# Cross-attention scores on two column tiles of the array

## The chip, the cores and the metric

The kernel runs on one core of a Trainium2 chip. The metric is the device time of one execution in microseconds (us), the median of several runs.

## The reference

One perceiver layer in float32 on `x` of 16 sequences x 64 tokens x 512: cross-attention to a context, then self-attention, then a feed-forward block with a mixture of small experts. Each adds to its input and takes a layer norm of it. The change is in the cross-attention:

```python
queries = (q @ Wq.T).reshape(B, Sq, 32, 128).transpose(0, 2, 1, 3)
keys    = (k @ Wk.T).reshape(B, Skv, 8, 128).transpose(0, 2, 1, 3)
values  = (v @ Wv.T).reshape(B, Skv, 8, 128).transpose(0, 2, 1, 3)
queries, keys = _rope(queries), _rope(keys)
keys, values = (jnp.repeat(t, 4, axis=1) for t in (keys, values))
scores = jnp.einsum('bhqd,bhkd->bhqk', queries, keys) * 128 ** -0.5
scores = jnp.where(causal, scores, finfo.min)
attn = softmax(scores); ctx = attn @ values; out = ctx @ Wd.T
```

The mask is causal, so of the context only the first 64 tokens matter.

## The kernel before

Everything lies in SBUF; the engines run hand-written programs that meet at semaphores. The cross-attention has 16 units: for each of 8 KV heads, two halves of 8 sequences. `phase(u, ...)` is one unit's program on an engine. A loop runs it 14 times (two to an iteration), unit 14 follows in a variant `"last"`, and unit 15 is taken apart among the work around it.

In unit `u`, TensorE (`pe`) first makes the scores (`scores_x`, chunk 0 and 1, four sequences each), then alternates the projections of unit `u+1` (`project`, in `proj_x`, `three`, L1110) with the rest of unit `u`: transposes of the softmax weights (`p_transposes`, L1149), weights times V (`pv_x`, L1156 and L1157), and at the end four output projections (`out_x`, L1110 too). Most products there are three `F32R` matmuls of values split in a high and a low part. The scores are plain float32: `qr` (queries after rope, 128 x 8 x 4 x 64: dimension, sequence, query head of the group, token) is the stationary operand, `kr` (keys) the moving one. A pair of query heads makes the 128 stationary columns, so that the result of one matmul has 128 partitions (2 heads x 64 query tokens) and 64 key columns. A chunk fills 512 columns of one PSUM bank, `sc[:, c, :]`:

```python
last = pe.matmul(sc[:, c, (2 * b + hp) * S:(2 * b + hp + 1) * S],
                 qr[h][:, bb, 2 * hp:2 * hp + 2, :], kr[h][:, bb, :],
                 start=True, stop=True)
```

After a chunk the semaphore `scored` goes up by one. VectorE (`dve`) adds the mask (`mask_max`, L787) and takes the maximum (L790), GpSimd (`pool`) subtracts it (L410), ScalarE (`act`) takes the exponential (L563), VectorE sums (L794), GpSimd normalises (L415) and raises `normed`, for which TensorE waits before `p_transposes`. The second chunk's exponential stands on ScalarE behind the copy of the next unit's first projection (`swap_halves`, L538 and L539). GpSimd also does the rope (L398, L403) and splits weights (L377); VectorE the rope's cosine part (L780), the output addition (L838) and the low parts of V (L804).

In the variant `"last"` the two chunks of unit 15 are scored between the output projections of unit 14 (after the second and after the fourth), while VectorE takes the statistics for the next layer norm (L735, L738) among its output additions.

In the self-attention behind it, `pv_s` (L1330) multiplies with 64 stationary columns, `vc[h][:, 2*c+b, t, :]`, for `t` = 0 and 1 in turn, into the partitions `64*t` to `64*t+63` of a bank. It also is plain float32, with 128 moving columns, eight records in a group, 32 groups. The matmuls around it are L1306 (scores), L1319 (transposes), L1261 (projections) and, in the last groups, L1402 (output projection).

Of the kernel before, what the change touches and what calls it, by code (L numbers as in the profile page):

```python
# [26 lines left out]
B, S, D = 16, 64, 512  # L27
# [32 lines left out]
def build(nc, x, ctxT, w_x, w_s, w_o, w_b, w_ag, w_eb, consts, bias_cols, bias_rows, b_thr, out):  # L60
    es = ExitStack()
    with es:
# [3 lines left out]
        def sb(stack, name, shape, dt=F32):  # L66
            return stack.enter_context(nc.sbuf_tensor(name, shape, dt))
# [27 lines left out]
        kr = [sb(xs, f"kr{i}", [P, HB, S]) for i in range(2)]  # L95
        qr = [sb(xs, f"qr{i}", [P, HB, REP, S]) for i in range(2)]
# [64 lines left out]
        def pb(name):  # L161
            return es.enter_context(nc.psum_tensor(name, [P, 2, 512], F32))
        pj, sc, tp, pv = pb("pj"), pb("sc"), pb("tp"), pb("pv")
# [925 lines left out]
        def _(pe):  # L1089
# [47 lines left out]
            def scores_x(u, h, c):  # L1137
                for b in range(4):
                    bb = 4 * c + b
                    for hp in range(2):  # L1140
                        last = pe.matmul(sc[:, c, (2 * b + hp) * S:(2 * b + hp + 1) * S],  # L1141
                                         qr[h][:, bb, 2 * hp:2 * hp + 2, :], kr[h][:, bb, :],
                                         start=True, stop=True)
                last.then_inc(scored, 1)

            def p_transposes(u, c):
# [48 lines left out]
            def phase(u, h, g, nxt):  # L1195
# [13 lines left out]

                pe.wait_ge(rope, 5 * u + 5)  # L1210
                scores_x(u, h, 0)
                scores_x(u, h, 1)
                project(0)
                project(1)
# [15 lines left out]
                for i in range(4):  # L1230
                    if i % 2 == 0:
                        pe.wait_ge(pv_lo, 2 * u + i // 2 + 1)
                    if i < 2:
                        pe.wait_ge(pj_act, XT * n + 5 + i)
                    pe.wait_ge(pj_dve, PD_LN1 + 4 * u + i - 1)
                    out_x(u, i)
                    if nxt == "last" and i in (1, 3):
                        if i == 1:
                            pe.wait_ge(rope, 5 * n + 5)
                        scores_x(n, 1, i // 2)  # L1240
# [179 lines left out]
            for n in range(N_SS):  # L1420
                v, c = n // SCH, n % SCH
# [79 lines left out]
            for i in range(NT):  # L1501
                pe.wait_ge(hw_done, i + 1)
                last = pe.transpose(sc[:, i // 4, (i % 4) * P:(i % 4 + 1) * P], hw[:, i, :], ident)
# [73 lines left out]
```

## Time and profile before

| | |
|---|---|
| median of 3 runs | 805.54 us (805.36 to 805.68) |
| span of the profiled execution | 802.9 us |
| TensorE matmuls busy | 780.4 us (97%) |
| TensorE weight loads busy | 643.9 us (80%) |
| VectorE, GpSimd, ScalarE busy | 511.5, 467.9, 390.6 us |
| mean granted clock of TensorE | 0.985 |

PE is TensorE's matmuls, PEld its loads of the stationary operand, DVE VectorE, ACT ScalarE, POOL GpSimd. The span goes from the first to the last instruction; the runs' time has 2.6 us more. A matmul's record is longer than the time after which the next one starts, since matmuls overlap in the array; so the distance of starts tells what one costs. A form such as `128*128 128x64` is rows and columns of the stationary operand, and then what is streamed past it. A plain float32 matmul shows as two loads and two matmul records (a transpose as one of each).

### The profile page before, as it was taken

Reading aid. Unit: us, or ns where it says so; the run is one execution under the profiler, and the core shown is the slowest. Engines: PE = TensorE matmul, PEld = TensorE weight load, DVE = VectorE, ACT = ScalarE, POOL = GpSimd, SP = SyncE. Lnnn points to the kernel's source line nnn. Section 1 sums busy time; section 2 is a strip of 40 time slices with the busy share of each in tenths; the row PEclk is TensorE's granted clock in tenths of the full one; section 3 lists DMA queues with packets and bytes.
Section 4 is the critical chain, followed back from the end, with each engine's and each line's share of the span. In section 5 each row is a group of like instructions: output and inputs, shape, how many; then the busy total and the mean of one; then the engine's idle time right before and its main releaser. Section 6 shows DMA issues by size and latency. Waiting matters only on the chain.

```text
span 802.9 us, 11770 instructions
## 1 busy us (share of the span) xinstructions
PE 780.4 (97%) x4112; PEld 643.9 (80%) x4112; DVE 511.5 (64%) x927; ACT 390.6 (49%) x692; POOL 467.9 (58%) x363
## 2 busy tenths in 40 slices
PE   6899999999999999999999999999799999999998
PEld 4688888888888888888888888888688777777786
DVE  6866465655655565565555566466857777779855
ACT  3546436453543735455373454537254666564220
POOL 4538546764754675485376458637543687865350
PEclk9889999999999999999999999999799999999999
DMA  8102101200210120030012003001101110001002
GB/s 296 53 2 78 53 1 52 78 0 0 78 52 0 52 78 0 0 97 34 0 52 78 0 3 124 3 0 41 40 1 52 40 51 2 2 19 63 14 1 105
DMA packets 11338, 34.09 MB, mean 42 GB/s; under 512 B 1456, under 2 KB 1584, under 8 KB 11312
## 3 DMA queue, kind: packets, MB, share of 16 engines
q1 hardware_dynamic: 11312, 33.75, 12.8%
q8 instruction: 16, 0.26, 0.1%
q14 instruction: 10, 0.08, 0.0%
HBM read 31.65 MB, written 2.10 MB: 42 GB/s over the span
## 4 chain that ended last, share of the span: by engine, by line
PE 90%; DVE 6%; issue 2%; ACT 1%; POOL 1%; DMA 1%; SPq 0%; ACTq 0%; POOLq 0%
PE pj L1110 53%; PE pj L1261 8%; PE sc L1141 7%; PE sc L1306 3%; PE pv L1330 2%; PE tp L1319 2%; PE pv L1156 2%; PE pv L1157 2%; PE tp L1149 2%; DVE sm L755 1%; PE pj L1402 1%; PE pj L1465 1%; PE tp L1134 1%; DVE al L857 1%; PE pv L1465 1%
## 5 line engine op out<-in xcount | busy, mean ns | idle before, releaser
L398 POOL TENSOR_TENSOR sw<-sw,cst 128x512 f32<-128x512 f32 x79 | 109.4, 1385 | 62.5 <-ACT sw L539 62.3
L410 POOL TENSOR_TENSOR sm<-sm,mx 128x512 f32<-128x512 f32 x64 | 67.3, 1052 | 133.9 <-DVE mx L790 133.9
L563 ACT ACTIVATE sm<-sm 128x512 f32<-128x512 f32 x64 | 40.5, 633 | 149.5 <-POOL sm L410 149.1
L538 ACT ACTIVATE sw<-pj 64x512 f32<-64x512 f32 x80 | 47.7, 596 | 127.0 <-DVE t L780 126.7
L1110 PE MATMUL pj<-xh,wqh 128*128 128x512 f32 x252 | 103.3, 410 | 0.0
L1110 PE MATMUL pj<-wdh,ch 128*128 128x512 f32 x256 | 101.8, 398 | 0.2 <-issue 0.2
L415 POOL TENSOR_TENSOR sm<-sm,rz 128x512 f32<-128x512 f32 x64 | 66.9, 1045 | 58.4 <-DVE rz L797 58.4
L1110 PE MATMUL pj<-wdh,cl 128*128 128x512 f32 x256 | 99.8, 390 | 0.0
L1110 PE MATMUL pj<-wdl,ch 128*128 128x512 f32 x256 | 99.7, 389 | 0.0
L1110 PE MATMUL pj<-xh,wql 128*128 128x512 f32 x252 | 99.6, 395 | 0.0
L1110 PE MATMUL pj<-xl,wqh 128*128 128x512 f32 x252 | 99.3, 394 | 0.0
L838 DVE TENSOR_TENSOR X<-X,pj 128x512 f32<-128x512 f32 x60 | 41.2, 686 | 73.7 <-PE pj L1110 73.2
L403 POOL TENSOR_TENSOR qr<-t,sw 128x512 f32<-128x512 f32 x63 | 82.0, 1301 | 4.9
L815 DVE TENSOR_TENSOR pt<-tp,pt 64x512 fp32r<-64x512 f32 x64 | 44.1, 689 | 57.0 <-ACT pt L557 56.5
L787 DVE TENSOR_TENSOR sm<-sc,cst 128x512 f32<-128x512 f32 x64 | 44.2, 690 | 42.7 <-PE sc L1306 22.2
L780 DVE TENSOR_TENSOR t<-pj,cst 128x512 f32<-128x512 f32 x80 | 55.1, 689 | 21.1 <-PE pj L1110 18.4
L1261 PE MATMUL pj<-xh,ws 128*128 128x512 f32 x192 | 67.8, 416 | 0.7 <-ACT xh L505 0.7
L1141 PEld LDWEIGHTS sc<-kr,qr 128*128 128x128 f32 x512 | 61.5, 197 | 4.6 <-DVE qr L889 3.4
L1141 PE MATMUL sc<-kr,qr 128*128 128x64 f32 x512 | 60.9, 278 | 3.1 <-DVE qr L889 3.1
L794 DVE TENSOR_REDUCE zs<-sm 128x8 f32<-128x512 f32 x64 | 43.5, 679 | 30.5 <-ACT sm L563 29.9
L377 POOL TENSOR_TENSOR wql<-raw,wqh 128x1024 fp32r<-128x1024 f32 x24 | 57.4, 2398 | 9.3 <-ACT wqh L505 9.1
L823 DVE TENSOR_TENSOR cl<-pv,ch 128x256 fp32r<-128x256 f32 x128 | 45.2, 415 | 24.6 <-ACT ch L568 24.6
(201 smaller groups left out, 1759.0 us busy)
## 6 DMA issues: line engine op xcount, KB each, us to landing
raw<-in_w_x SPq DMA_DIRECT2D x40, 512.0 KB, 4.0
qr<-in_ctxT SPq DMA_DIRECT2D x4, 512.0 KB, 7.1
X<-in_x SPq DMA_DIRECT2D x4, 512.0 KB, 7.5
raw<-in_w_s SPq DMA_DIRECT2D x4, 512.0 KB, 3.6
out<-X SPq DMA_DIRECT2D x8, 256.0 KB, 2.1
raw<-in_w_s SPq DMA_DIRECT2D x4, 256.0 KB, 3.1
raw<-in_w_o SPq DMA_DIRECT2D x2, 512.0 KB, 3.7
raw<-in_w_b SPq DMA_DIRECT2D x2, 512.0 KB, 6.2
```

Source lines behind the costliest of these rows:

```text
L377: pool.tensor_tensor(lo, src, hi.bitcast(F32), ALU.subtract).then_inc(wlo, 1)
L398: pool.tensor_tensor(sw[par][:, :].rearrange("p (b s) -> p b s", s=S), sw[par][:, :].rearrange("p (b s) -> p b s", s=S), rep(cst[:, C_SIN: ...
L403: pool.tensor_tensor(o, t1[par][:, :].rearrange("p (b s) -> p b s", s=S), sw[par][:, :].rearrange("p (b s) -> p b s", s=S), ALU.add).then_ ...
L410: pool.tensor_tensor(s3, s3, per_group(mx[:, c, :], 8), ALU.subtract).then_inc(subbed, 1)
L415: pool.tensor_tensor(s3, s3, per_group(rz[:, c, :], 8), ALU.mult).then_inc(normed, 1)
L538: act.activation(sw[par][0:64, :], src[64:128, :], ACT.Copy)
L780: dve.tensor_tensor(t1[par][:, :].rearrange("p (b s) -> p b s", s=S), pj[:, bank, :].rearrange("p (b s) -> p b s", s=S), rep(cst[:, C_COS: ...
L787: dve.tensor_tensor(s3, sc[:, c % 2, :].rearrange("p (n s) -> p n s", s=S), mask3, ALU.add).then_inc(masked, 1)
L823: last = dve.tensor_tensor(cl[:, r, cs].rearrange("p (b q) -> p b q", q=S), pv[:, :, :].rearrange("p a (b r q) -> p (a b) r q", b=2, r=REP ...
L1110: last = pe.matmul(o, w, r, start=(m == 0), stop=(m == n - 1))
L1141: last = pe.matmul(sc[:, c, (2 * b + hp) * S:(2 * b + hp + 1) * S], qr[h][:, bb, 2 * hp:2 * hp + 2, :], kr[h][:, bb, :], start=True, stop= ...
L1261: last = pe.matmul(pj[:, k % 2, :], ws[t][:, part // 2, i, c], (xl if part == 1 else xh)[:, i, tok], start=(m == 0), stop=(m == 3 * KT - 1))
```

## The change

Each score matmul on a pair of heads becomes two, one for each head `r`: 64 stationary columns, whose result goes to the partitions `64*r` to `64*r+63` of the same columns of the same bank. The data, the order of chunks and all semaphores stay.

```diff
                 for b in range(4):
                     bb = 4 * c + b
                     for hp in range(2):
-                        last = pe.matmul(sc[:, c, (2 * b + hp) * S:(2 * b + hp + 1) * S],
-                                         qr[h][:, bb, 2 * hp:2 * hp + 2, :], kr[h][:, bb, :],
-                                         start=True, stop=True)
+                        for r in range(2):
+                            last = pe.matmul(sc[64 * r:64 * r + 64, c, (2 * b + hp) * S:(2 * b + hp + 1) * S],
+                                             qr[h][:, bb, 2 * hp + r, :], kr[h][:, bb, :],
+                                             start=True, stop=True)
                 last.then_inc(scored, 1)
```

## Rows read from the trace of the kernel before

**Rows 1.** The page: engines (busy, share, records) and the chain that ended last

```profile
PE 780.4 (97%) x4112; PEld 643.9 (80%) x4112; DVE 511.5 (64%) x927; ACT 390.6 (49%) x692; POOL 467.9 (58%) x363
...
PE pj L1110 53%; PE pj L1261 8%; PE sc L1141 7%; PE sc L1306 3%; PE pv L1330 2%; PE tp L1319 2%; PE pv L1156 2%; PE pv L1157 2%; PE tp L1149 2%; DVE sm L755 1%; PE pj L1402 1%; PE pj L1465 1%; PE tp L1134 1%; DVE al L857 1%; PE pv L1465 1%
```

**Rows 2.** Waits of PE, whole span (total us, times, longest), the second of 16

```profile
PE sc L1141 <- DVE qr L889: 3.1, 1, 3.1
```

**Rows 3.** Records by line: count, duration ns min/median/max, first and last start

```profile
L1141 PEld LDWEIGHTS sc<-kr,qr x512: 187/192/337, 41.6 to 569.0; 128*128 128x128 f32 x171
L1141 PE MATMUL sc<-kr,qr x512: 217/275/422, 41.6 to 569.1; 128*128 128x64 f32 x171
...
L1330 PEld LDWEIGHTS pv<-pts,vc x256: 132/136/137, 617.2 to 740.1; 128*64 128x64 f32 x128
L1330 PE MATMUL pv<-pts,vc x256: 272/273/323, 617.2 to 740.2; 128*64 128x128 f32 x128
...
L1306 PE MATMUL sc<-kb,qm x128: 377/379/454, 591.3 to 730.0; 128*128 128x256 f32 x128
```

**Rows 4.** Timeline of PE around a unit's scores: start, length from first to last

```profile
114.03 0.39 PE L1110 MATMUL pj<-wdh,cl 128*128 128x512 f32 x1
114.26 3.68 PE L1141 MATMUL sc<-kr,qr 128*128 128x64 f32 x32
...
118.06 0.40 PE L1110 MATMUL pj<-al,wqh 128*128 128x512 f32 x1
```

**Rows 5.** Windows, records of L1330 alone; (x) counts those running in it

```profile
617.20:617.26 0.06, 0.04 (x2) 0.04 (x2) 1.00 0.00 0
617.26:617.37 0.11, 0.11 (x2) 0.11 (x4) 1.00 0.00 0
617.37:617.40 0.03, 0.03 (x4) 0.03 (x4) 1.00 0.00 0
617.48:617.52 0.04, 0.04 (x6) 0.04 (x4) 1.00 0.00 0
```

**Rows 6.** Timeline of PE around the last group of L1330

```profile
739.46 0.40 PE L1402 MATMUL pj<-woh,al 128*128 128x512 f32 x1
739.79 0.66 PE L1330 MATMUL pv<-pts,vc 128*64 128x128 f32 x8
...
740.72 0.39 PE L1402 MATMUL pj<-wol,ah 128*128 128x512 f32 x1
```

**Rows 7.** Windows, all engines: us, busy PE PEld DVE ACT POOL, granted clock, DMA

```profile
43.20:50.00 6.80, 6.80 (x27) 6.22 (x27) 5.88 (x10) 0.63 (x1) 2.29 (x3) 0.50 0.00 1
148.96:183.67 34.71, 34.71 (x181) 29.27 (x180) 18.81 (x33) 14.73 (x29) 18.49 (x15) 1.00 0.09 30
567.48:591.30 23.82, 19.62 (x93) 15.74 (x92) 15.48 (x28) 11.98 (x21) 7.58 (x7) 0.79 0.03 9
591.00:803.00 212.00, 205.00 (x1185) 161.31 (x1183) 157.21 (x330) 95.90 (x160) 123.40 (x104) 1.00 0.10 33
```

**Rows 8.** Timeline of DVE at the first chunk of unit 15

```profile
561.86 0.18 DVE L738 BATCH_NORM_AGGREGATE mv<-stats 128x2 f32<-128x6 f32 x1
562.14 0.69 DVE L787 TENSOR_TENSOR sm<-sc,cst 128x512 f32<-128x512 f32 x1
```

**Rows 9.** Timelines of DVE, POOL and PE in the unit at 148.96 us

```profile
149.16 0.69 DVE L838 TENSOR_TENSOR X<-X,pj 128x512 f32<-128x512 f32 x1 [1.33 <-PE pj L1110]
150.89 0.69 DVE L787 TENSOR_TENSOR sm<-sc,cst 128x512 f32<-128x512 f32 x1 [1.04 <-PE sc L1141]
...
155.17 1.05 POOL L415 TENSOR_TENSOR sm<-sm,rz 128x512 f32<-128x512 f32 x1
159.32 1.04 POOL L415 TENSOR_TENSOR sm<-sm,rz 128x512 f32<-128x512 f32 x1 [3.11 <-DVE rz L797]
...
158.13 0.60 PE L1149 MATMUL tp<-cst,sm 128*128 128x128 f32 x4
161.35 0.27 PE L1149 MATMUL tp<-cst,sm 128*128 128x128 f32 x1
```

## The prediction, as put down before the result

> **What bounds the kernel now.** I read the page first, then the chain of waits, the PE groups and their waits, then single stretches. The page and its chain say that TensorE is the bound: it is busy 97% of the span, and of the chain that ended last the projections (L1110) hold over half and the cross scores (L1141) 7% [rows 1]. The waits of PE are 16, of 3.2 us at most, nearly all at the start and around 570 us; the score line has one of 3.1 us, before the first unit, and none later [rows 2]. So inside the 15 regular units between 41 and 560 us every TensorE microsecond saved comes off the end, as long as the softmax chain keeps up. 802.9 us of the time is the span; the median of the runs is 805.54, so 2.6 us lie around the span, and the sum below takes its differences off both alike.
>
> **What the scores cost now.** A unit (one KV head, one half of the tokens) has 16 score matmuls. Each is f32 and shows as two loads and two matmul records, so the line has 512 records over 16 units [rows 3]. In a regular unit the last projection record before them starts at 114.03 us, the 32 score records start from 114.26 on, and the second projection record after them starts at 118.06 [rows 4]. That whole passage is 118.06 - 114.03 = 4.03 us. Inside it the 32 records last 3.68 us with 0.275 for the last one, so their pitch is (3.68 - 0.275)/31 = 0.110 us; leaving out the first, which had its load ready, it is 0.112. The moving side has only 64 columns. A record with 128 moving columns lasts 0.273 us, one with 256 0.379 [rows 3], so 128 columns stream in 0.106 us and 64 in 0.053. A pitch of 0.112 is therefore not the stream's: it is the load's of 128 columns. This is where there is something to win.
>
> **What the change does, step by step.** It issues twice the score matmuls (1024 records), each with a 64-column load, alternately on the left and the right half of the array. Nothing else is changed: no DMA, no wait, no PSUM bank, the same values in the same places, and one increment of the semaphore behind the last matmul of a chunk.
>
> 1. *The load.* 64 columns take 0.136 us as a record where 128 take 0.192 [rows 3], that is 0.056 less. From 0.112 the pitch of one half's loads becomes 0.056 to 0.057; the stream is 0.053, so both fit.
>
> 2. *Do the halves run side by side?* The same form already runs in the kernel: L1330 (self-attention times V) alternates the halves in the same way, f32, 64 columns loaded, 128 moving. The counts in narrow stretches show it: two matmuls and two loads start by 617.26, no matmul more until 617.37, two more by 617.40 and two more by 617.52 [rows 5]. Matmuls start in pairs, a pair per 0.109 us (0.66 us for eight records [rows 6] less 0.273 for the last is 0.38 for three steps; the first, into the halved array, takes 0.16, the others 0.11). One stream of 128 columns takes 0.106, so two streams run at once. The loads come in pairs as well. I take this for the new form: a pair per 0.057 us, 32 pairs a unit in place of 32 single records at 0.112. That the two halves would be side by side with 64 moving columns too is the step that the trace doesn't show. Its bounds are 0.053 (streams alone) and 0.113 (the loads of the halves one after the other, 2 x 0.0565).
>
> 3. *Entering and leaving the halved array.* From the last projection record before an L1330 group to the second record after it the trace has 739.46 to 740.72, 1.26 us for four pairs [rows 6]. Four streams of 0.106 are 0.43, and in projections without a switch the two records around would take 0.23 each. So some 0.4 us of it is switching. The Trainium skill says the same in a rule that speaks against this change (TensorEngine Tiling (Array Packing), Key Properties): changing the tiling mode drains TensorE. The trace agrees: 739.46 to 739.79 is 0.33 us where 0.23 is usual for such a record. It changes no number here, since the 1.26 us holds it.
>
> 4. *Sum of a unit.* 1.26 us for four pairs; each of these streams 64 columns instead of 128, 4 x (0.109 - 0.057) = 0.21 less; 28 more pairs at 0.057 are 1.60. That makes 2.65 us against 4.03: 1.38 us less per unit. With the pitch at its lower bound 0.053 it is 1.50 less.
>
> 5. *How many units.* 15 pass straight from projections into both chunks of scores and back. The first of them runs in a stretch at the lower clock, 1.2 GHz (granted clock 0.50 from 43.2 to 50.0 us [rows 7]). I count it as 1.38 like the others: if the stretch keeps its place, what is saved appears at its end at 2.4 GHz; at most it gives 2.8. The last unit's scores are written between the output projections (560.21 and 567.48), and there DVE is behind: its statistics end at 562.04, the mask of the scores starts at 562.14 [rows 8]. Earlier scores gain 0.1 us and no more; both half groups then leave PE waiting instead (0.5 us each).
>
> **Sum:** 15 x 1.38 + 0.1 = 20.8 us. 802.9 becomes 782.1, and 805.5 becomes 784.7.
>
> **What is late next.** In the unit at 148.96 us the first chunk's scores are masked at 150.89 by DVE and normalised by POOL until 156.22; PE asks for them at 158.13 [rows 9]: 1.9 us spare. The first chunk would be ready for the mask at about 150.2 (0.1 us for the switch, 0.11 to the second pair, 14 x 0.057, 0.22 for the last record), 0.7 earlier than now, while PE comes 1.38 earlier: 1.2 us remain. DVE is free in time, since its output addition ends at 149.85. The second chunk is normalised until 160.36 and wanted at 161.35: 1.0 spare. Its chain waits for the exponential behind ACT's copy of the next projection, which moves with PE, so 1.0 remains. The output addition that frees the bank for the second projection ends at 149.85, and that projection would start at about 153.9. Nothing in a unit comes to bind. DVE is busy 18.8 of 34.7 us of a unit, POOL 18.5, ACT 14.7 [rows 7], far from the new 33.3.
>
> **The rivals.**
>
> *The halves don't overlap (slower).* If the two loads of a pair go one after the other the pitch of a pair is 0.113 us, as dear as a whole record now, and the switch comes on top: 2.65 + 32 x 0.056 = 4.44 us, 0.41 more than now, times 16 gives 6.6 us, 812 us. It decides at a pitch of 0.057 + 1.38/32 = 0.100 us. For it: only four pairs in a row are ever seen. Against it: the loads that start in pairs [rows 5]. 0.09.
>
> *The instructions don't come fast enough (slower).* The new form wants two loads and two matmuls every 0.057 us, the densest seen is the same number per 0.109 [rows 5]; were 0.109 a limit of the issue, a unit would take 2.65 + 32 x 0.052 = 4.31 us, 0.28 more than now, x 16 = 4.5, 810 us. In rows 6 eight matmuls and eight loads start in 0.66 - 0.273 = 0.38 us without such a limit showing, but they may have been queued beforehand. 0.05. The Trainium skill has a rule of this sort (TensorE: Matmul & The Clock Gate, What happens when you issue a matmul): where the sequencer decodes matmuls in microcode it spends about 62 ns on each. By it a pair would take 0.124 us and the time would be an estimated 818; the trace's pairs at 0.109 don't agree with it, if they were not queued.
>
> *Partly overlapping.* Pairs hold their pitch only while the queue is full of them, or a conflict costs some 0.03 us each: 0.085 a pair makes a unit 2.65 + 32 x 0.028 = 3.55 us, 0.48 less than now, 15 x 0.48 = 7.2, 798 us. The range of such cases is 788 to 803. 0.12.
>
> *The change does nothing,* a pitch of a pair between 0.097 and 0.103: 0.03. For it there is no row, it is where the cases meet.
>
> *A softmax wait takes over.* PE would stop before the transposes of a chunk's weights (L1149) for POOL's normalised scores. The first chunk's would have to come 1.2 us later than worked out, the second's 1.0; each 0.1 us beyond that costs 1.5 us in all, and with 0.3 the time is 789. Against it is that every operation of the chain keeps its length: 0.02, 786 to 795.
>
> *The forecast:* 0.69.
>
> **The clock.** Through the stretch with 32 L1330 groups the granted clock is 1.00 [rows 7], so work on half arrays keeps 2.4 GHz. After the idle time near 570 us the clock is at 1.2 GHz for a while (0.79 on average from 567.48 to 591.30). There PE will idle about 1 us more than now. A longer slow stretch could cost up to 3 us, a luckier one give 2. This and the first unit are the main spread of the forecast itself: 781 to 788.
>
> **How the numbers follow.** The likeliest is 784.7. The lower end: pitch 0.053 (1.8 us less) and a lucky clock, 781. Upwards the range takes in the clock's 3 us and most of the partial cases, to 798. Left out are the slower cases (0.09 and 0.05), nothing (0.03) and a little of the partial. A measurement of this kernel tells about 0.2% (1.6 us) from nothing. Faster: 0.69 + 0.12 + 0.02 = 0.83; same 0.03; slower 0.14.
>
> **What the profile after would show.** The score line with 1024 records of a 64-column load, 0.136 us for the load and about 0.217 for the matmul; a unit's scores some 1.9 us from first to last start instead of 3.4; pairs of starts in narrow stretches, 0.057 us apart; a gap of about 0.1 us before and after; units 33.3 us apart instead of 34.7; no new PE wait for POOL's normalised scores in the units, some 1 us more idle PE near 570 us. The prediction is wrong if the starts of the score line come evenly at 0.055 us instead of two at a time, or if PE waits on POOL before the transposes at L1149.

## The result, and the profile after

The changed kernel takes 784.25 us (median of 4 runs, 783.46 to 785.41) against 805.61 us (4 runs). The ratio is 0.9732, with a 95% interval of 0.9717 to 0.9748. The forecast was 784.7 us, in a range of 781 to 798. The profiled execution took 783.46 us; its span is 781.6 us, 21.3 less than before.

These are lines of the changed kernel's page: the engines, and the chain of work that ended last, by line of the kernel (the line numbers below the edit are one higher: L1141 is now L1142, L1149 is L1150, L1261 is L1262, L1306 is L1307, L1330 is L1331):

```profile
PE 757.0 (97%) x4624; PEld 615.4 (79%) x4624; DVE 509.9 (65%) x927; ACT 388.7 (50%) x692; POOL 468.3 (60%) x363
...
PE pj L1110 53%; PE pj L1262 8%; PE sc L1142 4%; PE sc L1307 4%; PE pv L1331 2%; PE tp L1320 2%; PE pv L1157 2%; PE pv L1158 2%; PE tp L1150 2%; DVE sm L755 2%; PE pj L1403 1%; PE pj L1466 1%; PE tp L1134 1%; PE pv L1466 1%; PE tp L1466 1%
```

There are 512 matmul records more than in [rows 1], and 23.4 us less of PE's busy time. The score line has gone from 7% of the chain to 4%, and PE is still the bound. The score line's loads by themselves (count, duration in ns, first and last start), and an idle time before them:

```profile
L1142 PEld LDWEIGHTS sc<-kr,qr x1024: 132/138/228, 42.5 to 547.3; 128*64 128x64 f32 x171
...
  issue: 5.6, 16
```

1024 loads of 0.138 us have taken the place of 512 of 0.192 [rows 3]. The scores enter the halved array 17 times, once in each of 15 units and twice in the last. At the first entry the engine waits for DVE; before the other 16 the loads stand idle 0.35 us each, and the profile names nothing that they wait for ("issue"). The timeline of PE in a regular unit:

```profile
111.54 0.39 PE L1110 MATMUL pj<-wdh,cl 128*128 128x512 f32 x1
111.86 2.09 PE L1142 MATMUL sc<-kr,qr 128*64 128x64 f32 x64
113.87 0.50 PE L1110 MATMUL pj<-ah,wqh 128*128 128x512 f32 x1
114.21 0.39 PE L1110 MATMUL pj<-al,wqh 128*128 128x512 f32 x1
```

From here on, "passage" is the time from the start of the last projection record before a unit's scores to the start of the second one after them. Here it is 114.21 - 111.54 = 2.67 us, against 4.03 [rows 4]. Narrow windows at its start, for the records of the score line alone (the counts are of those running in the window):

```profile
111.83:111.90 0.07, 0.04 (x2) 0.05 (x2) 1.00 0.00 0
111.95:111.98 0.03, 0.03 (x4) 0.03 (x6) 1.00 0.00 0
112.00:112.03 0.03, 0.03 (x6) 0.03 (x5) 1.00 0.00 0
```

Two start at once, 0.11 us later two more, and from then on two every 0.058 us. The sum agrees: of the 2.09 us, 0.22 are the last record, 0.11 the first step and 0.007 the distance of the two starts of a pair, so that 1.75 are left for 30 steps from pair to pair.

The timelines show where the 21.3 us of the span were saved. They give the first score record of the first unit, of the second and of the fifteenth, then the first projection of the self-attention and the first of its scores. Before:

```profile
41.57 0.32 PE L1141 MATMUL sc<-kr,qr 128*128 128x64 f32 x1 [3.13 <-DVE qr L889]
...
79.56 0.22 PE L1141 MATMUL sc<-kr,qr 128*128 128x64 f32 x1
...
530.74 0.33 PE L1141 MATMUL sc<-kr,qr 128*128 128x64 f32 x2
578.17 0.79 PE L1261 MATMUL pj<-xh,ws 128*128 128x512 f32 x1 [0.69 <-ACT xh L505]
...
591.32 0.38 PE L1306 MATMUL sc<-kb,qm 128*128 128x256 f32 x1
```

After:

```profile
42.49 0.38 PE L1142 MATMUL sc<-kr,qr 128*64 128x64 f32 x2 [3.13 <-DVE qr L889]
...
78.53 0.28 PE L1142 MATMUL sc<-kr,qr 128*64 128x64 f32 x2
...
511.60 0.28 PE L1142 MATMUL sc<-kr,qr 128*64 128x64 f32 x2
557.33 0.79 PE L1262 MATMUL pj<-xh,ws 128*128 128x512 f32 x1 [0.69 <-ACT xh L505]
...
570.04 0.38 PE L1307 MATMUL sc<-kb,qm 128*128 128x256 f32 x1
```

| stretch | before | after | difference |
|---|---|---|---|
| to the first scores | 41.57 | 42.49 | +0.92 |
| first unit | 37.99 | 36.04 | -1.95 |
| the next 13 units | 451.18 | 433.07 | -18.11 (1.39 each) |
| unit 14, and unit 15 to the first self-attention projection | 47.43 | 45.73 | -1.70 |
| from there to the first self-attention scores | 13.15 | 12.71 | -0.44 |
| the rest (span 802.9 and 781.6) | 211.58 | 211.56 | 0.0 |

The 13 units give most of it. The two ends are mixed with the clock, and the first unit with new waits (below).

### The profile page after: what moved, and what is told of

It is laid out like the page before. It is cut to its first block, busy times and chain, and to the rows that moved or that the text cites. A ratio compares the mean times of both kernels' runs of the same rounds, so it can differ in the third digit from the quotient of the medians.

```text
span 781.6 us, 12794 instructions
## 1 busy us (share of the span) xinstructions
PE 757.0 (97%) x4624; PEld 615.4 (79%) x4624; DVE 509.9 (65%) x927; ACT 388.7 (50%) x692; POOL 468.3 (60%) x363
## 4 chain that ended last, share of the span: by engine, by line
PE 86%; DVE 6%; issue 3%; ACT 2%; POOL 2%; DMA 1%; SPq 0%; POOLq 0%; DVEq 0%; ACTq 0%
PE pj L1110 53%; PE pj L1262 8%; PE sc L1142 4%; PE sc L1307 4%; PE pv L1331 2%; PE tp L1320 2%; PE pv L1157 2%; PE pv L1158 2%; PE tp L1150 2%; DVE sm L755 2%; PE pj L1403 1%; PE pj L1466 1%; PE tp L1134 1%; PE pv L1466 1%; PE tp L1466 1%
## 5 line engine op out<-in xcount | busy, mean ns | idle before, releaser
L1262 PE MATMUL pj<-xh,ws 128*128 128x512 f32 x192 | 67.6, 415 | 0.7 <-ACT xh L505 0.7
L1110 PEld LDWEIGHTS pj<-wdh,ch 128*128 128x128 f32 x256 | 48.0, 188 | 12.9 <-ACT sw L539 3.0
L1110 PEld LDWEIGHTS pj<-wdh,cl 128*128 128x128 f32 x256 | 48.0, 188 | 10.3
```

The lines of the kernel that those rows point to most:

```text
L1110: last = pe.matmul(o, w, r, start=(m == 0), stop=(m == n - 1))
L1262: last = pe.matmul(pj[:, k % 2, :], ws[t][:, part // 2, i, c], (xl if part == 1 else xh)[:, i, tok], start=(m == 0), stop=(m == 3 * KT - 1))
```

## The experiments

Ten runs were made, each beside the kernel before: eight new kernels, and two of the kernels once more. In each of them the passages of the 14 units at the full clock differ by at most 0.01 us. So they tell more than the whole time, which is spread by 0.4 to 5.6 us between the executions of one kernel.

**Quarters instead of halves.** The same computation on four column tiles:

```diff
-                        for r in range(2):
-                            last = pe.matmul(sc[64 * r:64 * r + 64, c, (2 * b + hp) * S:(2 * b + hp + 1) * S],
-                                             qr[h][:, bb, 2 * hp + r, :], kr[h][:, bb, :],
-                                             start=True, stop=True)
+                        for r in range(4):
+                            last = pe.matmul(sc[32 * r:32 * r + 32, c, (2 * b + hp) * S:(2 * b + hp + 1) * S],
+                                             qr[h][:, bb, 2 * hp + r // 2, 32 * (r % 2):32 * (r % 2) + 32],
+                                             kr[h][:, bb, :], start=True, stop=True)
```

Expected: 

> Each score matmul is cut once more, into four of 32 stationary columns on the four quarters of the array, in turn. Theory (each column tile has its own loads and streams; the stream of 64 columns, 0.053 us, or the load paces it): a load of 32 columns takes 0.027 us, the stream stays 0.053, so four start together every 0.055 to 0.0585 us, a unit's scores cost the same as with halves, and the time is 783 to 785 us. Rival (the pitch of a pair, 0.0585 us, is the rate at which two loads and two matmuls can be issued, 0.0146 each): four loads and four matmuls take 0.117 us, a unit costs 32 x 0.0585 = 1.87 us more, 15 units 28 us, 812 us.

Measured: 783.12 us (783.03 to 783.38), ratio 0.972 (0.9704 to 0.9736). The rival's 812 us is far off: up to this rate the issue of instructions sets no limit, though a unit's scores now have 256 records of loads and matmuls in place of 128. The loads of this kernel's score line:

```profile
L1142 PEld LDWEIGHTS sc<-kr,qr x2048: 106/110/110, 41.8 to 545.7; 128*32 128x32 f32 x187
```

A load's record is now 0.110 us. From 128 to 64 columns it lost 0.054 us, from 64 to 32 another 0.028. So of the 0.192, 0.138 and 0.110 us, some 0.00085 us a column go with the columns (0.109, 0.054 and 0.027 us), and the rest is the same for all three.

**The order of the halves.** Same matmuls; first all of the left half in a chunk, then all of the right:

```diff
-                for b in range(4):
-                    bb = 4 * c + b
-                    for hp in range(2):
-                        for r in range(2):
+                for r in range(2):
+                    for b in range(4):
+                        bb = 4 * c + b
+                        for hp in range(2):
                             last = pe.matmul(sc[64 * r:64 * r + 64, c, (2 * b + hp) * S:(2 * b + hp + 1) * S],
```

Expected: 

> The same matmuls as after the change in another order: in a chunk first the 8 of the left half, then the 8 of the right half, so 16 records of one half stand in a row. Theory A (matmuls of one half may start ahead of earlier ones of the other half, as far as the queue reaches): part or all of the overlap stays; if it reaches over the 32 instructions of a half, 784 us. Theory B (starts keep the written order, so only neighbours on different halves overlap): 64 records of 0.0585 us less a few overlaps, 3.6 us in place of 1.87, 15 units add 26 us, 810 us, slower than before the change.

And in blocks of two matmuls (`for r` between `for b` and `for hp`). Expected: 

> The same matmuls in blocks: two matmuls (four records) on the left half, then two on the right. Theory A (starts may run ahead over the other half's records): 784 us as after the change. Theory B (starts keep the written order): of eight records two slots are shared, 48 slots of 0.0585 us a unit in place of 32, 0.94 us more, 15 units 14 us, 798 us.

Measured: halves apart 803.03 us (802.03 to 803.37), ratio 0.9968 (0.9955 to 0.998); blocks of two 784.97 us (784.03 to 785.17), ratio 0.9743 (0.9727 to 0.976). PE in a unit with the halves apart:

```profile
113.76 0.39 PE L1110 MATMUL pj<-wdh,cl 128*128 128x512 f32 x1
114.08 3.41 PE L1142 MATMUL sc<-kr,qr 128*64 128x64 f32 x64
117.41 0.51 PE L1110 MATMUL pj<-ah,wqh 128*128 128x512 f32 x1
117.76 0.39 PE L1110 MATMUL pj<-al,wqh 128*128 128x512 f32 x1
```

and in blocks of two:

```profile
110.68 0.39 PE L1110 MATMUL pj<-wdh,cl 128*128 128x512 f32 x1
111.00 2.13 PE L1142 MATMUL sc<-kr,qr 128*64 128x64 f32 x64
113.06 0.50 PE L1110 MATMUL pj<-ah,wqh 128*128 128x512 f32 x1
113.40 0.39 PE L1110 MATMUL pj<-al,wqh 128*128 128x512 f32 x1
```

The passages are 4.00 and 2.72 us. The strict order of theory B fails: blocks of four records overlap almost wholly (0.05 us a unit lost). But with sixteen records of one half in a row most of the overlap is gone, so of theory A only the weaker form holds: matmuls start ahead over a short reach. How far it goes is read with the next run.

**One half only.** Both heads go to the left half, one over the other; the upper 64 partitions of the scores are left out:

```diff
-                            last = pe.matmul(sc[64 * r:64 * r + 64, c, (2 * b + hp) * S:(2 * b + hp + 1) * S],
+                            last = pe.matmul(sc[0:64, c, (2 * b + hp) * S:(2 * b + hp + 1) * S],
```

Expected: 

> The changed kernel with both heads' matmuls on the left half of the array: 64 columns each, the same loads and streams, but the second head's scores overwrite the first's in the partitions 0 to 63, and those of 64 to 127 are never written (this part of the computation is left out). Theory (the whole gain is the two halves side by side; the shorter load alone gives a pitch of 0.0585 us per record): 64 records cost 3.74 us in place of 1.87, 15 units add 28 us to the changed kernel's 784.3, 812 us, slower than before. Rival (a good part of the gain is the shorter load, and records of 64 columns on one half follow each other at the stream's 0.053 us or faster): 807 us or less.

Measured: 812.39 us (809.41 to 812.88), ratio 1.0069 (1.0043 to 1.0095), and in a unit:

```profile
114.83 0.39 PE L1110 MATMUL pj<-wdh,cl 128*128 128x512 f32 x1
115.15 3.94 PE L1142 MATMUL sc<-kr,qr 128*64 128x64 f32 x64
119.03 0.50 PE L1110 MATMUL pj<-ah,wqh 128*128 128x512 f32 x1
119.36 0.39 PE L1110 MATMUL pj<-al,wqh 128*128 128x512 f32 x1
```

The passage is 4.53 us, and the pitch of a single record (3.94 - 0.22 - 0.11)/62 = 0.058 us, which is that of a pair after the change. So the whole gain is the two halves side by side; the same shorter loads on one half made the kernel 0.7% slower. With the halves apart a unit is 0.53 us shorter than this. A unit has three borders between left and right blocks, so 0.53/3/0.058 = 3 records overlap at each. The trace with the halves apart shows it at the first border (score records alone). On one half, where records of 0.222 us start 0.058 apart, four or five run at a time; here it is seven:

```profile
115.00:115.04 0.04, 0.04 (x7) 0.04 (x5) 1.00 0.00 0
```

An instruction of the other half is thus brought forward over some three records, and not over sixteen.

**One chunk on halves.** The first chunk as before the change, the second as after it (`if c == 0` around the two forms). Expected: 

> Only the second chunk of a unit is scored on halves, the first stays on the whole array, so there is one switch in and out per unit as after the change, and half of its work. The passages measured so far are 4.03 us with 32 records at 0.112 and 2.67 us with 32 pairs at 0.0585; without the records 0.46 and 0.80 us, so switching costs 0.34 us a unit. Theory (switching has a fixed price): 0.80 + 16 x 0.112 + 16 x 0.0585 = 3.53 us, 0.50 less than before, 15 units 7.5 us, 798 us. Rival (no price of its own, the gain goes with the number of pairs): half of the 21.4 us, 795 us.

Measured: 795.61 us (794.48 to 798.42), ratio 0.9886 (0.9861 to 0.9911), which is 794.1 to 798.1 us and doesn't part 798 from 795. The passage does better:

```profile
145.48 0.39 PE L1110 MATMUL pj<-wdh,cl 128*128 128x512 f32 x1
145.71 1.89 PE L1142 MATMUL sc<-kr,qr 128*128 128x64 f32 x16
147.53 1.15 PE L1147 MATMUL sc<-kr,qr 128*64 128x64 f32 x32
148.61 0.50 PE L1110 MATMUL pj<-ah,wqh 128*128 128x512 f32 x1
148.95 0.39 PE L1110 MATMUL pj<-al,wqh 128*128 128x512 f32 x1
```

The passage is 3.47 us, where a fixed price of 0.34 gives 3.53 and a gain in proportion (4.03 + 2.67)/2 = 3.35. So switching has a price of its own, 3.47 - 0.46 - 16 x 0.112 - 16 x 0.0585 = 0.28 us (0.46 is the passage before the change without its records, two projection records of 0.23). The other 0.06 of the 0.34 fits an advantage that the scores have before the change at their start, and still have in this run: the second record starts 0.055 us after the first in place of 0.112, as if the first load were done early.

**Once more,** the changed kernel and the quarters. Expected of the changed kernel: 

> The changed kernel once more, beside the three that follow. Both theories: 784 us, 21.0 to 21.5 us less than before.

Of the quarters: 

> The kernel with four column tiles once more, in five rounds. Theory (halves are paced by the load of 64 columns, a pair per 0.0585 us; quarters by the stream, four per 0.0559): the passages of the earlier trace are 2.587 us against 2.673, 15 units x 0.086 = 1.3 us less than halves, 782.9 us. Rival (the difference of the first run was one of the clock's slow stretches, 20.5 us of them against 23.9): the same time as halves.

Measured: 784.32 us (783.73 to 785.48), ratio 0.9733 (0.9716 to 0.9749), and 782.41 us (782.2 to 783.73), ratio 0.9712 (0.9696 to 0.9728). The intervals overlap. The passages don't: 2.67 us again with halves, and with quarters

```profile
110.17 0.39 PE L1110 MATMUL pj<-wdh,cl 128*128 128x512 f32 x1
110.49 1.99 PE L1142 MATMUL sc<-kr,qr 128*32 128x64 f32 x128
112.41 0.51 PE L1110 MATMUL pj<-ah,wqh 128*128 128x512 f32 x1
112.75 0.39 PE L1110 MATMUL pj<-al,wqh 128*128 128x512 f32 x1
```

2.58 to 2.59. The 0.09 us a unit are 1.3 us in all; the rest of the 1.9 between the medians may be clock. The pitch of four records is (1.99 - 0.22 - 0.02 - 0.08)/30 = 0.056 us (0.02 for the three that start beside the last group's first, 0.08 for the first step). With the load half as long the pitch fell by some 0.003 us only. In both kernels, and in the one before, it lies 0.003 to 0.004 above the longer of load and stream: 0.112 above a load of 0.109, 0.058 above one of 0.054, 0.056 above the stream's 0.053. That fits halves paced by the load and quarters by the stream. But the two lie too close together for these runs to show more.

**Fewer switches.** If a switch costs 0.3 us, the 32 groups of `pv_s` in the self-attention pay it 32 times. In the next two runs they go two at a time:

```diff
-                pv_s(n)
+                if n % 2:
+                    pv_s(n - 1)
+                    pv_s(n)
```

Expected: 

> The changed kernel, and in the self-attention the groups of pv_s (on halves as before) run two at a time: after every second chunk of scores both, so that there are 16 groups of 16 records for 32 of 8. Theory (entering and leaving the halved array costs 0.30 us a group there, whatever the group's length): 16 x 0.30 = 4.8 us less, 779.4 us. Rival (the first of the two comes one chunk later, some 4 us, and the selection on DVE and what hangs on it comes late): PE waits more at the end of that stage, and the time is 784 us or more.

With quarters in the scores too: 

> Four column tiles for the scores and the groups of pv_s two at a time. Theory (both gains are of TensorE's own time and add): 1.3 + 4.8 us less than the changed kernel, 778.1 us. Rival as for the run before: no less than quarters alone, 783 us.

Measured: 803.73 us (801.88 to 806.85), ratio 0.9976 (0.9961 to 0.999), and 805.18 us (800.91 to 806.48), ratio 0.9975 (0.9958 to 0.9992). The rival's waits came, and cost much more than it said. The timeline of the first run shows the largest:

```profile
607.57 1.09 PE L1331 MATMUL pv<-pts,vc 128*64 128x128 f32 x16
608.28 0.41 DVE L958 TENSOR_SCALAR osel<-pv,cst,bcol 128x128 f32<-128x128 f32 x1 [2.34 <-PE pv L1331]
608.99 1.72 DVE L945 COPY vc<-tp 64x256 f32<-64x256 f32 x4
...
610.81 0.41 PE L1320 MATMUL tp<-cst,sm 128*128 128x128 f32 x2 [2.14 <-issue]
```

DVE stood idle 2.34 us for the first `pv_s` of the pair, the copy of the next tile's V stands behind that on DVE, and PE's transposes wait for the copy. The profile puts their 2.14 us down to "issue"; they begin 0.10 us after the copy's end at 610.71. It happens 7 times, 15 us in all.

Time was lost in the clock too. After three of these waits PE's granted clock is at half for a while, from 630.5 to 633.9, from 651.0 to 654.3 and from 671.5 to 674.8 us. From the windows of PE and from the chain that ended last, the first of these stretches, and nine projection records before it and in it:

```profile
630.50:633.90 3.40, 3.40 (x10) 0.50 0.00 0
...
611.44 2.09 PE pj L1262 x9
...
630.28 3.56 PE pj L1262 x9
```

The traces of the changed kernel have no such stretch between the groups of `pv_s`; that of the second of these two runs has six.

The last run puts the copy ahead of the selection:

```diff
+                if c == 3 and v + 1 < NSU:
+                    if v == 0:
+                        dve.wait_ge(zeroed, 4)
+                    vc_copy(v + 1)
                 if n == 0:
                     for i in range(NT + 4, 2 * NT):
                         ln_lo(i)
                 else:
                     select_out(n - 1)
-                if c == 3 and v + 1 < NSU:
-                    if v == 0:
-                        dve.wait_ge(zeroed, 4)
-                    vc_copy(v + 1)
```

Expected: 

> As the run before with four column tiles and pv_s in twos, and on DVE the copy of the next tile's V (vc_copy, L945) stands before the selection (select_out) in the last chunk of each tile. The theory of the loss in the runs with pv_s in twos: in each of 7 tiles DVE waits 2.3 us for the first pv_s of the pair, the copy of V (1.7 us) stands behind it, and PE's transposes wait 2.2 us for that copy; with the copy ahead these waits go, and of the switches 16 x 0.30 = 4.8 us are gained: 782.4 - 4.8 = 777.6 us. Rival (the selection itself and the mask behind it come 1.4 us late, and the chain to the next weights holds PE anyway): 783 to 800 us.

Measured: 784.59 us (784.16 to 785.8), ratio 0.9733 (0.9718 to 0.9748). The cause of the large loss is shown, since it went with the copy's place, and the slow stretches with it. But the gain didn't come, and the time is the rival's. The waits of PE now begin with

```profile
PE tp L1320 <- POOL sm L415: 5.4, 10, 1.1
```

for normalised weights, which take 0.2 us with the changed kernel. The mask stands on DVE behind the selection, which is late; that this is what delays the weights is argued from the order and not tested.

The switches did become cheaper. From the last record of the scores to the second one of the transposes PE takes 1.06 us with a group of eight records between, 1.50 with sixteen and 0.33 with none, which makes 2 x 1.06 - 1.50 - 0.33 = 0.30 us saved for each two groups, 4.8 in all. But counted in the same way, from start to start, the waits cost some 8 us. The profile's 5.4 is less because it counts from the end of a record, while the next would have started before that end. The stage from its first transposes (592.19 us with quarters, 593.71 here) to its last `pv_s` record (716.52 and 721.21) is accordingly 3.2 us longer. The quarters alone, with `pv_s` as it was, stay the fastest kernel measured.

## Why the prediction was right

*TensorE bounds the units.* This held. The distance of units fell from 34.71 to 33.32 us; 33.3 was predicted. The prediction misread [rows 2] on the way: its 16 are kinds of wait, and 3.2 us the total of two. It also passed over 3.6 us of waits behind 591 us. Neither enters the sum.

*The pitch (steps 1 and 2).* Predicted were 0.057 us a pair, measured 0.058. That the halves run side by side with 64 moving columns, which the trace before didn't show, is shown by the windows and by the run on one half, where the same records cost 0.058 each. That the load paces the halves fits the quarters, where a load half as long takes the pitch down by 0.003 only; it is not shown apart from that.

*The switch (step 3).* Carried over from L1330's groups it was right: from 1.26 us for four pairs there the sum made 2.65 for 32 pairs, and they took 2.67. The rule of the Trainium skill (TensorEngine Tiling (Array Packing), Key Properties), that a change of mode drains TensorE, gives no size. The run with one chunk does: some 0.28 us for the way in and out.

*The sum of a unit (step 4).* The passage lost 4.03 - 2.67 = 1.36 us, where 1.38 was predicted; a whole unit is 1.39 shorter. The 0.03 between are spread over the other records of the unit.

*The ends (step 5).* The first unit gained 1.95 us and started 0.92 later, 1.03 in all for the 1.38 of the sum. One cause is that the stretches at 1.2 GHz moved, which the granted clock of the changed kernel (0.54 and 0.62 below) shows:

```profile
18.00:29.00 11.00, 9.32 (x29) 7.13 (x29) 8.97 (x18) 5.89 (x10) 5.20 (x4) 0.54 0.14 32
41.50:46.00 4.50, 3.51 (x65) 3.44 (x66) 4.42 (x8) 2.03 (x4) 0.00 (x0) 0.62 0.01 2
```

Before, the first window has 0.69, and the lower clock after the first scores lasts from 43.2 to 50.0 [rows 7] where now it is over by 46. More was lost ahead and less behind. The other cause is that PE, back at the full clock sooner, now waits in this unit, for POOL's normalised weights and for ACT's copy (and once more for ACT, 0.17 us at 52.66):

```profile
51.84 0.65 PE L1150 MATMUL tp<-cst,sm 128*128 128x128 f32 x4 [0.24 <-POOL sm L415]
...
67.39 0.50 PE L1110 MATMUL pj<-wdh,ch 128*128 128x512 f32 x1 [0.50 <-ACT sw L539]
```

Before, it was busy through the whole of the first unit. Step 5, which took the saving as coming through whole, didn't have this.

The last unit was the one term of the sum that was mis-sized: 0.1 us was predicted, and 1.70 - 1.39 = 0.3 came. Step 5 took the mask as starting no sooner than the end of the statistics' last record (0.18 us long). Now the mask starts at 541.33 and that record at 541.23, a distance of 0.10, where it was 0.28 before [rows 8]; that is 0.18 of the 0.3. Another 0.10 is only where the count begins: the first score record comes 0.32 us behind the last projection record (511.28), and came 0.22 behind it before. Another 0.44 us came after 557 us, from where the slow stretch ended. All this lies within the spread that was given.

*The slack (what is late next).* PE and POOL in a unit of the changed kernel, the one whose scores begin at 145.16 us:

```profile
152.86 0.60 PE L1150 MATMUL tp<-cst,sm 128*128 128x128 f32 x4
156.08 0.60 PE L1150 MATMUL tp<-cst,sm 128*128 128x128 f32 x4
```

```profile
150.60 1.04 POOL L415 TENSOR_TENSOR sm<-sm,rz 128x512 f32<-128x512 f32 x1 [0.39 <-DVE rz L797]
154.23 1.04 POOL L415 TENSOR_TENSOR sm<-sm,rz 128x512 f32<-128x512 f32 x1 [2.59 <-DVE rz L797]
```

The first chunk is normalised at 151.64 and wanted at 152.86, with 1.2 us to spare as predicted. The second is normalised at 155.27 and wanted at 156.08, with 0.8 to spare where 1.0 was predicted. DVE's cosine part (150.54) now stands behind the first chunk's sum and reciprocal, where before it waited for PE (from 155.05 to 155.63), so that the second chunk's chain doesn't quite move with PE. Near 549 us PE idles 1.57 us for POOL, where it had 0.62, the microsecond that was expected.

*The rivals.* No overlap: it is what the run on one half gives, 812.4 us for the 812 worked out, so its price was right. Issue: refuted by the quarters, with eight records (four loads, four matmuls) in 0.056 us. The rule of the Trainium skill (TensorE: Matmul & The Clock Gate, What happens when you issue a matmul) of some 62 ns for each matmul decoded in microcode doesn't apply in these runs: the quarters start 128 matmuls in 1.77 us, 14 ns each. Partial overlap: it came only with another order of the matmuls. A softmax wait: there is none in the 14 units at the full clock, whose slack is above. In the first unit it did come, 0.24 us with the changed kernel and 1.3 to 1.6 in four of the other runs (blocks of two, both runs with quarters alone, `pv_s` in twos on the changed kernel). The prediction had named such a wait as a sign of being wrong. It comes in one unit only, so it costs that much once, and not in all 15 units as the rival reckoned.

## What to carry to other kernels

Where matmuls stream fewer columns than they load, compare the pitch of starts with the stream's time. If the load sets it, column tiles can hide loads behind one another. But matmuls of different tiles must alternate closely in the program, and a group must be long enough to pay some 0.3 us for the switch. Here 32 pairs saved 1.4 us. Each saves 0.054 us, so an estimate from these runs puts the even point near six pairs. On one half alone the same matmuls cost 0.5 us a unit more than before. A group that already ran in the wanted form elsewhere in the trace, together with the records on either side of it, gave the price of a unit to 0.02 us. And before work is moved to save a switch, look at what stands behind its consumer: `pv_s` in twos took away 4.8 us of switches, and the kernel became 19 us slower, through the place of one copy on DVE and the slow clock that followed.

## What the runs showed of the hardware that wasn't expected

- Matmuls of one column tile start ahead of earlier ones of another, but over a short reach: blocks of four records overlap nearly wholly (2.72 us a passage against 2.67), blocks of sixteen by about three records at each border (4.00 us against 4.53 with none).
- With four tiles, 128 matmul and 128 load records start within 1.77 us without a sign of an issue limit; the four of a group start 0.007 us apart.
- With f32, the record of a load grows by 0.00085 us a column at a granted clock of 1.00 (0.192, 0.138 and 0.110 us for 128, 64 and 32 columns). So 64 loaded columns cost 0.054 us, and 64 streamed ones 0.053: loads on halves and a stream of 64 columns are just in balance.
- Waits of 2.1 us, one to each tile of the self-attention, were enough to bring PE's granted clock down to half three times in one run (from 630.5, 651.0 and 671.4 us) and six times in another; with these waits gone it stayed at 1.00 through that stage.
